# A graph layer stack on one core: the rows ahead of attention are normalised by ScalarE instead of VectorE

## What is computed

```python
xn = _layernorm(x)
x = x + _L0_gnn_ref(xn, src, dst, deg, ...) + _L0_mix_ref(xn[None], ...)[0]   # SAGE layer, linear attention
x = x + _L0_ffn_ref(_layernorm(x)[None], ...)[0]                             # softmax attention
# _L0_ffn_ref, with x the normalised rows:
routing_input = x.mean(axis=1)
logits = jax.nn.relu(routing_input @ r_w1 + r_b1) @ r_w2 + r_b2
sel = jnp.argmax(jax.nn.softmax(logits, axis=-1), axis=-1)      # which of three weight sets
# then attention with 8 heads and the chosen wq, wk, wv, wo
```

## Time and profile before

| | us |
|---|---|
| median of 3 runs | 1616.06 (1613.36 to 1617.21) |
| profiled execution, its own time | 1617.9 |
| its span in the trace | 1616.1 |
| TensorE busy in the span | 1475.7 (91%) |
| VectorE, ScalarE, GpSimd busy | 680.1, 370.9, 463.3 |
| mean granted clock of TensorE | 0.968 of full speed |

### The profile page before, as it was taken

How to read it: one execution, slowest core, us unless ns; L and a number is a source line. 1 busy time by engine, 2 the same in 40 slices (tenths; PEclk the granted TensorE clock), 3 DMA queues, 4 the chain that set the end, 5 groups by cost and what they waited for, 6 DMA issues and landing times.

```text
span 1616.1 us, 18934 instructions
## 1 busy us (share of the span) xinstructions
PE 1475.7 (91%) x7301; PEld 976.5 (60%) x7301; DVE 680.1 (42%) x1242; ACT 370.9 (23%) x612; POOL 463.3 (29%) x449
## 2 busy tenths in 40 slices
PE   5999977999998799999999998999998679998996
PEld 3546744544557587666666744678866476554553
DVE  7422047788525624466666340424252651111110
ACT  2210002212020133344444405102151201000010
POOL 3100021002410121388888818102010121332111
PEclk9999999999999899999999999999999799999998
DMA  6000010004100022111110073003001947999995
GB/s 208 0 0 0 1 54 1 14 14 168 34 5 0 7 90 92 50 25 25 33 33 18 1 164 92 0 1 131 0 1 63 402 148 275 392 384 396 411 409 219
DMA packets 41675, 176.17 MB, mean 109 GB/s; under 512 B 6293, under 2 KB 6879, under 8 KB 39666
## 3 DMA queue, kind: packets, MB, share of 16 engines
q1 hardware_dynamic: 37561, 169.21, 29.2%
q0 software_dynamic: 3712, 5.40, 1.5%
q10 hardware_dynamic: 313, 0.35, 0.1%
HBM read 153.33 MB, written 19.05 MB: 107 GB/s over the span
## 4 chain that ended last, share of the span: by engine, by line
PE 74%; DVE 9%; DMA 8%; SPq 4%; issue 2%; POOL 1%; ACT 1%; another core or an unknown queue 0%; POOLq 0%; DVEq 0%; ACTq 0%
PE psum L1034 8%; PE psum L1025 6%; PE psum L1320 6%; PE psum L1191 5%; PE psum L1566 5%; PE psum L1048 4%; PE psum L1056 4%; SPq L431 4%; DMA arena<-in_w_down 4%; PE psum L1546 4%; PE psum L1306 3%; PE psum L1411 3%; DMA arena<-in_w_in 2%; PE psum L1308 2%; PE psum L1171 2%; PE psum L1180 2%
## 5 line engine op out<-in xcount | busy, mean ns | idle before, releaser
L703 POOL TENSOR_TENSOR arena<-arena 125x420 f32<-125x420 f32 x192 | 178.6, 930 | 28.0 <-ACT arena L933 0.9
L1566 PE MATMUL psum<-arena 128*39 128x512 f32 (+1 forms) x704 | 157.1, 603 | 10.4 <-DMA arena<-in_w_down 8.1
L1860 DVE TENSOR_REDUCE neg_max<-psum 125x1 fp32r<-125x1250 f32 x80 | 116.7, 1459 | 101.0 <-PE psum L1274 53.2
L933 ACT ACTIVATE arena<-psum 125x420 f32<-125x420 f32 x240 | 107.5, 521 | 124.3 <-PE psum L1308 124.3
L1566 PEld LDWEIGHTS psum<-arena 128*39 128x39 f32 (+1 forms) x704 | 52.2, 117 | 109.3 <-issue 104.8
L1025 PE MATMUL psum<-arena 128*128 128x512 f32 (+1 forms) x288 | 103.8, 522 | 3.9 <-DMA arena<-in_w_in 3.2
L1320 PE MATMUL psum<-arena 125*64 125x210 f32 x960 | 102.7, 349 | 0.0
L1546 PEld LDWEIGHTS psum<-arena 128*128 128x128 f32 (+1 forms) x704 | 95.6, 190 | 10.6 <-issue 7.0
L1546 PE MATMUL psum<-arena 128*128 128x156 f32 (+1 forms) x704 | 97.7, 301 | 4.5 <-DVE arena L2072 3.5
L787 POOL DMA_INDIRECT out_x<-arena,idx x32 | 44.9, 1402 | 198.6 <-DMA out_x<-arena,idx 111.0
L1306 PE MATMUL psum<-arena_r 128*125 128x420 f32 x240 | 92.5, 385 | 0.7 <-ACT arena_r L922 0.7
(11 more groups left out here) (372 smaller groups left out, 2458.1 us busy)
## 6 DMA issues: line engine op xcount, KB each, us to landing
arena<-in_w_down SPq DMA_DIRECT2D x96, 768.0 KB, 19.9
arena<-in_w_up SPq DMA_DIRECT2D x32, 682.5 KB, 19.8
arena<-in_w_down SPq DMA_DIRECT2D x32, 512.0 KB
a_spill<-arena SPq DMA_DIRECT2D x1, 5468.8 KB
adj<-a_spill SPq DMA_DIRECT2D x1, 5468.8 KB
bc<-k_dram SPq DMA_DIRECT2D x16, 312.5 KB, 4.2
gw<-in_gw SPq DMA_DIRECT2D x2, 2048.0 KB, 9.1
arena<-in_wkqv SPq DMA_DIRECT2D x1, 3072.0 KB, 18.6
```

The costliest lines, as they stand in the source:

```text
L703: pool.tensor_tensor(SUMS[rnd % 2], SUMS[rnd % 2], PT[s % P_RING], ALU.add).then_inc(sum_added, 1)
L933: act.activation(PT[s % P_RING], ring(step_entry(s))[:, 0:QW], ACT.Exp).then_inc(ring_done, 1)
L1566: ins = pe.matmul(o[64 * j:64 * j + CAP, :], ACTT[g % 2][0:w, f, at:at + CAP], DN[e % 5][0:w, f], start=f == 0, stop=f == FT - 1)
L1860: dve.tensor_reduce(neg_max[:, k:k + 1], max_bank[:, 0:N], AX.X, ALU.max, negate=True).then_inc(max_ready, 1)
```

## The change

The ten normalisations of "ffn" go from VectorE to ScalarE. ScalarE computes identity(scale * x + bias), with scale the factor and bias minus mean times factor, both read per partition. GpSimd makes the bias in a new tile ln_nm, in two instructions after the power, so rstd("ffn", g) is written out; done() makes GpSimd wait for the end of its own instruction. In ScalarE's program the calls for groups 0 and 1 stand ahead of all copies of turned rows, and the one for group 2 between the copies of group 0 and those of group 1 (ahead_of_last is called when g is 1).

```diff
+        ln_nm = sb("ln_nm", [TOK, TILES])
...
-            for g in range(3):
+            for g, (lo, hi) in enumerate(GROUPS):
                 rstd("sage", g)
-                rstd("ffn", g)
+                pool.wait_ge(ln_mv, LN_TILES["ffn", g])
+                pool.tensor_scalar(ln_rs[:, lo:hi], ln_mv_t[:, lo:hi, 1], LN_EPS, None, ALU.add).then_inc(ln_eps, 1)
+                pool.wait_ge(ln_eps, LN_NUMBER["ffn", g] + 1)
+                done(pool.tensor_tensor(ln_rs[:, lo:hi], ln_rs[:, lo:hi], minus_half[:, lo:hi], ALU.pow))
+                done(pool.tensor_tensor(ln_nm[:, lo:hi], ln_mv_t[:, lo:hi, 0], ln_rs[:, lo:hi], ALU.mult))
+                pool.tensor_scalar(ln_nm[:, lo:hi], ln_nm[:, lo:hi], -1.0, None, ALU.mult).then_inc(ln_rstd, 1)
...
-            def drain_turned(stage, dst, affine=None, sums=None):
+            def drain_turned(stage, dst, affine=None, sums=None, ahead_of_last=None):
 
                 n = ROW[stage]
                 for g, (lo, hi) in enumerate(GROUPS):
+                    if g == 1 and ahead_of_last:
+                        ahead_of_last()
                     for c in range(C):
...
-            drain_turned("ffn_t", XLT, sums=part_sum)
+
+            def normalise_ffn(g):
+
+                act.wait_ge(ln_rstd, LN_NUMBER["ffn", g] + 1)
+                for t in range(*GROUPS[g]):
+                    act.activation(XL[:, t], X[:, t], ACT.Identity, scale=ln_rs[:, t:t + 1],
+                                   bias=ln_nm[:, t:t + 1]).then_inc(ln_out, 1)
+
+            normalise_ffn(0)
+            normalise_ffn(1)
+            drain_turned("ffn_t", XLT, sums=part_sum, ahead_of_last=lambda: normalise_ffn(2))
...
                     if g and t == lo:
                         sage_out(g - 1)
-                    if g and t == lo + 1:
-                        normalise("ffn", g - 1, X, XL)
                 stats("sage", g, H, lambda t: dve.wait_ge(rows_free, ROW["sage"] + 2 * t + 2))
             sage_out(2)
-            normalise("ffn", 2, X, XL)
```

## The result

The changed kernel takes 1618.91 us as the median of 20 runs (1615.51 to 1622.99), the one before, on the same chips, 1615.37 (1612.48 to 1618.29): a ratio of 1.0024, 95% interval 1.0016 to 1.0033, so 2.6 to 5.3 us slower, +3.5 between the medians. Forecast were 1618.7 and +2.6.

The account below looks back on a forecast made before the run. The bound was the chain of waits from the SAGE rows to the last copy of turned rows: ScalarE's start on group 2 -0.74, copy order +3.35, together +2.6 on 1616.06, so 1618.7; range 1615.2 to 1620.8, main case 1617.4 to 1619.5.

Parts of the forecast that it names:

- upper end of +3.4: High bound of the main case: product as dear as a power (+0.48) and more GpSimd disturbance (+0.3).
- the forecast's own line of 3.2 us: About 0.2%, what a measurement of this kernel tells from no change; slower than that had 0.25.
- VectorE's side: Without group 1's normalising the last SAGE statistics start 2.03 us earlier; group 0's is worth nothing.
- GpSimd's side: Two added steps for group 2 cost 0.62 us on the path, disturbance by VectorE 0.68 more.
- The disturbance by L1817 and L1818: VectorE's heavy-count copies slow each of GpSimd's four group 2 steps by 0.17, 0.68 us; upper end 1.0.
- ScalarE's side: Activations 0.70 us apart, 0.80 each; group 2's pair takes 1.50 against VectorE's 1.01; group 0's copies begin at 554.2.
- The order of the copies: Group 2's normalising ahead of group 1's copies leaves eight copies behind it; from its start to last copy 6.78 against 3.43.
- Group 1's copies do hold: Denies the rival that group 1's copies cost nothing behind group 2's normalising: -0.9 us, 1615.2, chance 0.10.
- No table load: Denies the rival that a 1.28 us load precedes ScalarE's first new activation: at best +1.3, 1617.4, chance 0.05.
- group 0 wasn't late: Denies the rival that group 1's normalising holds group 0's copies beyond 560.06, each microsecond over adding one; chance 0.03.
- the clock rival: TensorE's full clock returns later, lower level reaching into L1243's key products: 1.7 us more, +4.3, 1620.4, chance 0.14.

Follow-up runs that it names:

- The pieces: Changed kernel with each of VectorE's two heavy-count instructions cut into five of 250 columns; ratio 1.0023 to the kernel before.
- the changed kernel with the tile last: Changed kernel with ln_nm declared behind all other tiles, so that none of them moves; ratio 1.0018 to the kernel before.
- The exchange of the order: Changed kernel with group 2 normalised behind group 1's copies in ScalarE's queue; ratio 1.0001 to the kernel before, last copy at 14.87 us.
- the undisturbed GpSimd: Changed kernel with VectorE's heavy counts held until GpSimd's last step for group 2; ratio 1.0019 to the kernel before, last copy at 16.25 us.
- The two shared kernels: Kernel before with group 1's tiles 4 and 5 normalised on VectorE, 6 and 7 on ScalarE; ratio 1.0011, and 0.9998 with ln_nm declared last.
- the one that moves a single call: Kernel before with VectorE normalising group 1 behind the last SAGE statistics, no ScalarE or new factors; ratio 0.9995, last copy at 12.84 us.

## Why the prediction was right, and where it missed

**The number, and the luck in it.** 1618.91 against the forecast 1618.7 looks closer than it is. The forecast added +2.6 to a median of 1616.06; in the comparison the kernel before stood at 1615.37, and the change cost +3.5. The sum was 0.9 us too small: as a difference the result is just past the upper end of +3.4, and the absolute time lies within that case's 1617.4 to 1619.5 because the kernel before was 0.7 faster this time. By the forecast's own line of 3.2 us, +3.5 is on the slower side, to which it gave 0.25; the interval reaches below that line.

**VectorE's side: right.** 2.03 us forecast, 2.02 in the profile. Group 0's normalising was worth nothing.

**GpSimd's side: the mechanism was right, the size wrong.** This is the term that missed. The two added steps cost 0.20 and 0.25 with gaps of 0.08 and 0.09, together 0.62, as forecast (none of VectorE's heavy-count work beside them); the product is not priced like a power. The disturbance by L1817 and L1818 was put at 4 x 0.17 = 0.68 us and measured 1.12 + 0.59 = 1.71, on the first two steps alone. I had taken 0.17 from a place where VectorE ran instructions of 0.47 us. The pieces show what that row could not: GpSimd waits for the end of the VectorE instruction under way, and L1817 is 1.42 long there, so the price is to be read from the length of one VectorE instruction, not from a ratio. Nor do "both lose": VectorE's two instructions took 1.42 and 0.86 beside GpSimd, 1.45 and 0.86 before. And not every VectorE instruction holds GpSimd: while VectorE took the last SAGE halves out of their banks and formed statistics (555.26 to 557.90), GpSimd's four steps for group 1 (from 555.44) took 0.23, 1.03, 0.20 and 0.24. With VectorE idle the power had taken 1.03 too, and the last two 0.20 and 0.25 for group 0 (at 528.44 and 528.72). The Trainium skill, GPSIMD Engine Reference, in its table of specifications, says that the SBUF interfaces are shared with VectorE and that instructions with two SBUF inputs or in a 2-port mode contend; the trace agrees, 1.34 us for 0.22 beside a subtraction of two SBUF tiles, and the forecast's upper end of 1.0 for all four steps was too low.

**ScalarE's side: right.** Forecast were a distance of 0.70, 0.80 for one and 1.50 for the pair; measured 2.93 for four and 1.52 for two, so 0.705 apart. There is no load of a table with them: the first new activations start on GpSimd's signal, and the profile still has four loads of 1.28 us. Group 0's copies began 4.30 us behind the mark (forecast 554.2 - 549.92 = 4.28).

**The order of the copies: right.** From ScalarE's start on group 2 to the last copy the sum had 6.78; the profile has 573.68 - 567.14 = 6.54, the changed kernel with the tile last 6.78 (17.96 at the last copy, its four steps 1.33, 1.31, 0.20 and 0.25). In the second TensorE's granted clock stayed at 0.50 from 564.90 to 568.90, in the first it was 0.66 over the like stretch, 570 to 574. That the 6.78 came out to the hundredth is luck in two terms. The 0.82 between two copies, read as "back to back", was a wait for TensorE: its four transposes at 557.22 took 0.65 us and ended at 557.87, just ahead of the copy at 557.90. Back to back, group 2's first copy came 0.67 behind group 1's last, and the second 0.77 behind that, where 0.82 and 0.63 had been laid out. The exchange of the order, which gave back 2.85 us, shows that this was the larger cost, as forecast; the undisturbed GpSimd gave back 1.47.

So the forecast of +2.6 at the last copy, with 1.03 added for GpSimd, is +3.6; measured were +3.41 and, with the lower clock, 17.96 - 14.31 = +3.65. Behind the last copy two things differed: in the changed kernel's profile the router's eight products took 1.02 us instead of 1.84, at a granted clock of 1.00 instead of 0.50, the load of the key weights took 5.04 instead of 4.89, and the first key product stood at +2.73. With the tile last they took 1.84 and it stood at 28.92 - 25.17 = +3.75. The measured +2.6 to +5.3 holds both.

**The rivals.** Group 1's copies do hold, so -0.9 is out. The clock did not reach down into the key products: the 48 took 9.47 us for 9.49. No table load; group 0 wasn't late (it ended at 563.62, 3.5 us ahead of need). Slower by over 0.2% had 0.25, but only 0.10 of it for what happened, the sum itself ending above +3.2; 0.14 stood on the clock rival, which didn't come. With the measured size of the disturbance the sum is +3.6 and crosses that line by itself.

**What stays open.** The two shared kernels' stretches are 1.6 us shorter than before, but their ratios are 1.0011 and 0.9998. The stages outside the stretch vary by microseconds between the profiles, and 12 runs don't settle a tenth of a per cent. No version is shown to beat the kernel before; the one that moves a single call (0.9995, 0.9981 to 1.0010) is a candidate, no more.

## What to carry to other kernels

Work that is moved to an idle engine joins that engine's queue, so look first at what stands behind it: here the larger part of the price was four copies that had always been ready early. Look next at what the relieved engine does instead, since it now runs beside helpers that had the memory to themselves; the wait it may impose on a step is as long as its longest single instruction. And before giving work away, ask whether the same engine has a wait into which it fits: the moved call took 1.47 us off the stretch without giving work to another engine.

## What the runs showed of the hardware

GpSimd's small steps in SBUF were held to the end of a VectorE instruction with two SBUF inputs: 1.34, 1.33 and 1.33 us for 0.22 in three kernels, beside an instruction of 1.42 us. Beside a multiplication by a scalar of 0.86 us a power took 1.30, 1.30 and 1.31 for 0.71. Beside VectorE instructions that read a bank or form statistics they took what they take alone. Cut into pieces of 250 columns, the same VectorE work cost them 0.37 us in sum.
A product of 125x2 or 125x4 on GpSimd took 0.20 us, where the power of the same shapes took 0.71 and 1.03.
The first two wide copies behind ScalarE's own normalising stood 0.56 us apart (568.56 and 569.12), against 0.82 in the run of copies before, where the second waited for its block.
32 products of one unchanged stage took 9.61 us at a granted clock of 0.83 and 8.30 at 1.00, in kernels whose programs are the same up to there.
